# Attention row sums as pairs of slabs added on GpSimd, and value products in four query quarters: a change to a conditioned attention kernel

## What is computed

```
h   = gamma * ((x - mean) / sqrt(var + eps) * ln_g + ln_b) + beta     # gamma, beta: cond @ Wg.T + bg, cond @ Wb.T + bb
q, k, v = split(h @ Wqkv.T + bqkv)                                   # 16 heads of 32
att = softmax(q @ k.T) / sqrt(512)
h1  = concat(att @ v) @ Wp.T + bp + x
out = (the same conditioned layer norm of h1) + h1
```

## Time and profile before

| | us |
|---|---|
| median of three runs | 1585.34 |
| lowest, highest | 1584.9, 1586.55 |
| profiled execution | 1583.32 |
| its span, first to last instruction | 1581.7 |
| mean granted TensorE clock | 0.976 of full speed |

### The profile page before, as it was taken

The page is one execution under the profiler, slowest core; times in us unless marked ns, Lnnn a source line. Parts: engine busy times, 40 slices in busy tenths (PEclk is TensorE's granted clock), DMA queues, the critical chain, the costliest instruction groups (busy, mean ns, idle before and its releaser), DMA issues.

```text
span 1581.7 us, 28876 instructions
## 1 busy us (share of the span) xinstructions
PE 1468.6 (93%) x8756; PEld 832.5 (53%) x8756; DVE 945.9 (60%) x1697; ACT 655.1 (41%) x794; POOL 426.7 (27%) x523
## 2 busy tenths in 40 slices
PE   6998999999999999999999999999999999999733
PEld 4886645555554656555555556555444444344332
DVE  5336666565656566665656666565666665666145
ACT  3221444444444444444444444344444444445300
POOL 2442201111111233131423323121313231323357
PEclk9999999999999999999999999999999999999966
DMA  6799563645434676656454575556334242423142
GB/s 215 178 173 186 135 77 97 92 111 70 109 86 85 162 108 154 72 149 91 118 126 94 160 97 160 56 141 95 95 82 111 67 121 54 123 58 92 52 113 87
DMA packets 211534, 175.98 MB, mean 111 GB/s; under 512 B 102644, under 2 KB 177396, under 8 KB 211480
## 3 DMA queue, kind: packets, MB, share of 16 engines
q1 hardware_dynamic: 209176, 167.96, 50.6%
q0 software_dynamic: 2304, 7.34, 1.2%
HBM read 115.13 MB, written 59.31 MB: 110 GB/s over the span
## 4 chain that ended last, share of the span: by engine, by line
PE 79%; DVE 7%; SPq 4%; issue 3%; DMA 3%; POOL 2%; ACT 1%; POOLq 1%; DVEq 0%; ACTq 0%
PE ps_o L673 19%; PE ps_a L638 16%; PE ps_st L653 11%; PE ps_w L545 9%; PE ps_o L670 9%; PE ps_w L602 8%; DVE half_max L993 5%; PE ps_st L602 3%; SPq L401 1%; PE ps_o L545 1%; PE ps_w L591 1%; DMA scale_t<-rcp_scratch 1%; PE ps_a L632 0%; POOL oT_s L1159 0%; SPq L356 0%
## 5 line engine op out<-in xcount | busy, mean ns | idle before, releaser
L993 DVE TENSOR_REDUCE half_max<-ps_a 128x1 f32<-128x512 f32 x1024 | 689.2, 689 | 484.0 <-PE ps_a L638 478.6
L809 ACT ACTIVATE p<-ps_st 128x1024 f32<-128x1024 f32 x512 | 521.9, 1025 | 499.4 <-PE ps_st L653 495.0
L670 PE MATMUL ps_o<-p,v_head 128*32 128x512 f32 x2048 | 490.2, 600 | 0.0
L673 PE MATMUL ps_o<-p,v_head 128*1 128x512 f32 x2048 | 483.5, 593 | 0.0
L638 PE MATMUL ps_a<-k_stack,q_stack 96*128 96x512 f32 x1024 | 429.4, 432 | 23.7 <-DVEq L1001 7.2
L653 PE MATMUL ps_st<-q_stack,k_stack 98*128 98x512 f32 x1024 | 328.7, 402 | 6.7 <-DMA q_stack<-max_rows 6.7
L638 PEld LDWEIGHTS ps_a<-k_stack,q_stack 96*128 96x128 f32 x1024 | 190.5, 188 | 256.1 <-DVE half_max L993 122.6
L653 PEld LDWEIGHTS ps_st<-q_stack,k_stack 98*128 98x128 f32 x1024 | 188.7, 191 | 40.8 <-issue 10.5
L602 PEld LDWEIGHTS ps_w<-hT_s,wqkv_s 128*128 128x128 f32 x1056 | 146.4, 188 | 47.4 <-issue 36.9
L602 PE MATMUL ps_w<-hT_s,wqkv_s 128*128 128x256 f32 x1056 | 158.0, 285 | 0.0
L673 PEld LDWEIGHTS ps_o<-p,v_head 128*1 128x1 f32 x2048 | 69.8, 82 | 154.8 <-issue 154.8
(11 more groups left out here) (86 smaller groups left out, 1017.9 us busy)
## 6 DMA issues: line engine op xcount, KB each, us to landing
qk_scratch<-qkT_s SPq DMA_DIRECT2D x108, 256.0 KB, 2.4
q_stack<-qk_scratch SPq DMA_DIRECT2D x192, 128.0 KB, 3.0
k_stack<-qk_scratch SPq DMA_DIRECT2D x192, 128.0 KB, 3.3
v_scratch<-v_parts SPq DMA_DIRECT2D x32, 264.0 KB, 10.7
v_head<-v_scratch SPq DMA_DIRECT2D x64, 132.0 KB, 2.2
x_tile<-in_x SPq DMA_DIRECT2D x32, 256.0 KB, 5.3
gq_s<-gain_bias_scratch SPq DMA_DIRECT2D x16, 512.0 KB, 4.9
att_scratch<-o_stage SPq DMA_DIRECT2D x128, 64.0 KB, 1.6
```

Of the source, the lines that this page charges most:

```text
L670: pe.matmul(ps_o[HD * e:HD * e + HD, :], v_head[:, s, k, 0:HD], p32[:, k, e * 512:(e + 1) * 512], start=(k == 0), stop=(k == 7))
L673: mm = pe.matmul(ps_o[64 + HD * e:65 + HD * e, :], v_head[:, s, k, HD:VP], p32[:, k, e * 512:(e + 1) * 512], start=(k == 0), stop=(k == 7))
L809: nc.scalar.activation(p32[:, k, :], scores, ACT.Exp).then_inc(exp_done, 1)
L993: V.tensor_reduce(half_max[:, s % 2, item:item + 1], ps_a[:, parity, :], AX.X, ALU.max).then_inc(a_used, 1)
```

## The change

It does the following.
1. **Row sums.** The column of sqrt(512) leaves V (`VP` goes, V is stored with 32 columns) and is a tile of its own, `root_s`. POOL adds slab `2j` to slab `2j + 1` in place in `p32`, 128 x 1024 (`pair_add`), four times a head, once the products of both slabs with V are done, at steps given by `PAIR_ADD_STEP`. PE multiplies each added pair with `root_s` (`pair_sums`) in a bank of its own, `ps_s`, four products of 256 queries. Pair 0's sums are at step `k = 7`, pairs 1, 2 and 3 at `k = 1, 3, 5` of the next head, ahead of the products with V.
2. **Values.** `weighted` makes four products of 256 queries a slab at the four partition groups of `ps_o`, where `sums` made two of 512 for V and two of 512 for the sums. Both slabs of a burst wait once.
3. **Scores.** `ps_st` has three banks of 512 columns where it had four. The two halves of a slab are separate: the first is issued where both were, the second after the second piece and all `a_item`s of the step, right before the burst. ACT takes two exponentials of 512 columns. A half waits for the exponential of the half three before (`ST_AFTER`), but the second half of a new head's first slab waits for the last half of the head before.
4. **Copies and stores.** `take_out` (256 columns, `k = 2`) and `take_sums` (256 columns, `k = 6`) for one copy of 512; four DMAs for the output, and four for the sums at `k = 7`.
5. **Tables.** Output projection at steps 21, 22, 25, 26 (was 23, 24, 27, 28), layer norm statistics of the second tile and POOL's norms earlier, reciprocals at step 9, output loads at step 12, residual loads at step 1.

```
-OUT_STAGE = {23: (0, 1), 24: (0, 2), 27: (1, 1), 28: (1, 2)}
-LN_STEP = {5: 0, 13: 1}
-OUT_STATS_STEP = {27: 0, 31: 1}
-NORM_SCALE_STEP = {7: 0, 15: 1}
-NORM_GAIN_STEP = {9: 0, 17: 1}
-RESIDUAL_STEP = {9: 0, 13: 1}
+OUT_STAGE = {21: (0, 1), 22: (0, 2), 25: (1, 1), 26: (1, 2)}
+LN_STEP = {5: 0, 9: 1}
+OUT_STATS_STEP = {25: 0, 29: 1}
+PAIR_ADD_STEP = {0: 2, 2: 3, 4: 0, 6: 1}
+RESIDUAL_STEP = {3: 0, 4: 1}
+NORM_SCALE_STEP = {7: 0, 11: 1}
+NORM_GAIN_STEP = {8: 0, 12: 1}
+OUT_NORM_STEP = {15: 0, 16: 1}
+OUT_LOW_STEP = {19: 0, 20: 1}
 OUT_SCALE_STEP = {27: 0, 31: 1}
-OUT_FINISH_STEP = {29: 0, 31: 1}
+OUT_FINISH_STEP = {28: 0, 31: 1}
-RECIP_STEP = 7
-RECIP_STORE_STEP = 8
-OUT_LOAD_STEP = 10
-OUT_NORM_STEP = {13: 0, 15: 1}
-OUT_HIGH_STEP = {16: 0, 18: 1}
-OUT_LOW_STEP = {18: 0, 20: 1}
+RECIP_STEP = 9
+RECIP_STORE_STEP = 10
+RESIDUAL_LOAD_STEP = 1
+OUT_LOAD_STEP = 12
+OUT_HIGH_STEP = {17: 0, 18: 1}
...
+        ST_BANK = [0, 1, 2] * 5 + [1]
+        ST_AFTER = [r - 3 for r in range(15)] + [13]
+        ST_AFTER[0:3] = [12 - 16, 15 - 16, 14 - 16]
...
-                need(pe, exp_done, 32 * g + 8 * s + k - 1)
-                for e in range(2):
-                    mm = pe.matmul(ps_st[:, k % 2, e, :], ...)
-                mm.then_inc(st_ready, 1)
+                need(pe, exp_done, 64 * g + 16 * s + ST_AFTER[2 * k + e] + 1)
+                pe.matmul(ps_st[:, ST_BANK[2 * k + e], :], ...).then_inc(st_ready, 1)
...
-                for e in range(2):
-                    pe.matmul(ps_o[HD * e:HD * e + HD, :], v_head[:, s, k, 0:HD], p32[:, k, e * 512:(e + 1) * 512], ...)
-                for e in range(2):
-                    mm = pe.matmul(ps_o[64 + HD * e:65 + HD * e, :], v_head[:, s, k, HD:VP], p32[:, k, e * 512:(e + 1) * 512], ...)
-                mm.then_inc(pv_done, 1)
+                for e in range(4):
+                    mm = pe.matmul(ps_o[HD * e:HD * e + HD, 0:QW], v_head[:, s, k, :], p32[:, k, e * QW:(e + 1) * QW], ...)
+                if k % 2:
+                    mm.then_inc(pv_done, 1)
+            def pair_sums(g, s, j):
...
+                pe.wait_ge(pair_added, 16 * g + 4 * s + j + 1)
+                for e in range(4):
+                    mm = pe.matmul(ps_s[HD * e:HD * e + 1, 0:QW], root_s[:], p32[:, 2 * j + 1, e * QW:(e + 1) * QW],
+                                   start=(j == 0), stop=(j == 3))
+                mm.then_inc(sum_done, 1)
...
+                n, k = 64 * i + 2 * step, step % 8
+                freed = 16 * i + 4 * (step // 8) + k // 2 - 3
+                for e in range(2):
+                    act.wait_ge(st_ready, n + e + 1)
+                    if e == 0:
+                        need(act, sum_done if k % 2 else pair_added, freed)
+                    nc.scalar.activation(p32[:, k, e * 512:(e + 1) * 512], ps_st[:, ST_BANK[2 * k + e], :], ACT.Exp
+                                         ).then_inc(exp_done, 1)
...
+            def pair_add(g, s, j):
+                pool.wait_ge(pv_done, 16 * g + 4 * s + j + 1)
+                G.tensor_tensor(p32[:, 2 * j + 1, :], p32[:, 2 * j, :], p32[:, 2 * j + 1, :], ALU.add).then_inc(pair_added, 1)
...
                 for step in range(32):
+                    s, k = step // 8, step % 8
+                    if k in PAIR_ADD_STEP:
+                        j = PAIR_ADD_STEP[k]
+                        if j < 2:
+                            pair_add(i, s, j)
+                        elif not (first and s == 0):
+                            pair_add(i - (s == 0), (s - 1) % 4, j)
```

More of the change, by code:

```diff
@@ L479, in iteration @@
                             store_row(u + 1, (s + 1) % 4)
+                        if k == 7 and not (first and s == 0):
+                            store_sums(u - 1, (s + 3) % 4)
+                        if outs and step == RESIDUAL_LOAD_STEP:
+                            for a in range(2):
+                                load_residual(pair, a)
                         if step == RECIP_STORE_STEP and not first:
@@ L515, in _ @@
             for half in range(2):
[L516 removed]
+                sp.wait_ge(att_out[half], 256 * ITERS)
             for a in range(2):
@@ L719, in iteration @@
                             a_item(*use)
[L720 to L723, removed]
+                        after = (i, s, k + 1) if k < 7 else (i + (s + 1) // 4, (s + 1) % 4, 0)
+                        if last and (s, k) == (3, 7):
+                            after = None
+                        if after:
+                            turned_scores(*after, 0)
                         piece(step - 1, 1)
@@ L726, in iteration @@
                             a_item(*use)
+                        if after:
+                            turned_scores(*after, 1)
+                        before = (i - (s == 0), (s - 1) % 4)
                         if k % 2:
+                            behind = not (first and s == 0)
+                            if k == 7:
+                                pair_sums(i, s, 0)
+                            elif behind:
+                                pair_sums(*before, (k + 1) // 2)
                             for j in (k - 3, k - 2):
                                 if j >= 0:
-                                    sums(i, s, j)
-                                elif not (first and s == 0):
-                                    sums(i - (s == 0), (s - 1) % 4, j + 8)
+                                    weighted(i, s, j)
+                                elif behind:
+                                    weighted(*before, j + 8)
                         piece(step, 0)
@@ L743, in _ @@
             iteration(ITERS - 1, False, True, last=True)
-            for k in (6, 7):
-                sums(ITERS - 1, 3, k)
+            for k in range(6, 8):
+                weighted(ITERS - 1, 3, k)
+            for j in range(1, 4):
+                pair_sums(ITERS - 1, 3, j)
             for m in range(END, ITERS):
@@ L831, in iteration @@
                     if k == 2 and not (first and s == 0):
+                        take_out(4 * i + s - 1, (s + 3) % 4)
+                    if k == 6 and not (first and s == 0):
                         take_sums(4 * i + s - 1, (s + 3) % 4)
```

96 lines of the change are left out of this document (54 added, 42 removed).

## The result

| | us |
|---|---|
| changed kernel, median of 4 runs (lowest, highest) | 1666.42 (1661.9, 1670.76) |
| kernel before, in the same runs | 1585.94 (1584.9, 1587.51) |
| ratio, 95% interval | 1.0506 (1.0474 to 1.0538) |
| span of the profiled execution, before and after | 1581.7, 1660.2 |

The change makes the kernel 5.1% slower, 80 us. The forecast was no change (1583), with a range that ended at 1619.

A forecast was written before the change was run, and what follows sets the result against it. PE was taken to set the time, though not wholly, with DVE's reductions pacing some pairs. From 1583.3 profiled, -78.7 + 50 + 10 + 3 + 13.5 = -2, median 1583 us; own range 1572 to 1596, with rivals 1545 to 1619.

The forecast's parts named there:

- POOL's adds: 256 additions of 128 x 1024 on POOL: 2.37 us each, POOL's busy time from 427 to some 1034 us.
- Burst: PE's products with V and row sums: 1.42 us to the next load, 0.43 saved in each of 256 bursts.
- DVE's pace: Step pairs without a long tile piece: limited by DVE's reductions, period 4.06 us, 0.21 saved in each of 127.
- What is left of the gain after exponentials and smaller parts: Whole kernel without POOL's losses: 78.7 us gain, less 10 for exponentials and 3 for the output projection's start.
- C: Iterations 11 to 15, with output projections alone: 75.8 us before, some 76 forecast, including 3.9 lost to POOL.
- so I take no change: Reciprocals two steps later, but Q and K stacks issued before them: no change, 2 us either way in five iterations.
- Exponentials: ACT's two exponentials of 512 columns: hidden except at step 7 of 11 iterations, 0.9 us each, 10 us lost.
- POOL late after iterations with outputs: PE waits at step 3 for POOL's late add: 5.1 us six times, 3.9 five times, 50 us lost.
- the tail: End of last iteration: 37.3 us from step 21's burst to the last product's end, 13.5 us later than before.
- POOL keeps up: Rival, 20%: an add on POOL may run at the one-input rate, 1.35 us, giving 1545 us.
- The adds are slow: Rival, 14%: POOL's adds take 3.3 us, giving 1619 us; it decides from an add of 2.5 us on.
- Issue bounds the burst: Rival, 12%: 24 loads 0.06 us apart make PE's burst 1.57 us, giving 1614 us.

The follow-up runs named there:

- e11: Kernel before, with the maxima's high and low parts made by DVE reductions, nothing else changed: 1594.3 us, ratio 0.9979.
- e8: Changed kernel with all DVE work on the maxima between SBUF operands done by reductions, POOL's adds kept: 1595.5 us, ratio 1.0020 to the kernel before.
- e7: Changed kernel without POOL's adds, PE summing both slabs of each pair itself: 1644.4 us, ratio 1.0345 to the kernel before.
- e1: Changed kernel without POOL's adds or waits for them, half of each row sum left out: 1518.2 us, ratio 0.9565 to the kernel before.
- e6: Changed kernel, maxima's high part by a reduction, second output tile's last two POOL instructions behind next iteration's step 0 add: 1661.5 us, ratio 1.0449.
- e9: e8 with the second output tile's last two POOL instructions moved behind the add of step 0 of the next iteration: 1550.9 us, ratio 0.9736.
- e10: e9 with those two POOL instructions moved further, behind the add of step 2: 1533.9 us, ratio 0.9607 to the kernel before.

## Why the prediction was wrong

**The step that failed** is in the part on POOL's adds: "I take 2.37, as most of DVE's work in the loop reads PSUM". The sentence asks how DVE slows POOL. It was right on that (2.38). It never asks how POOL slows DVE. The 128 small instructions per kernel between SBUF operands were in the trace, and one of them took 1.28 us where its median was 0.17, which is one POOL instruction. The groups by line that I read had them too, with means of 0.22 and 0.24 us. I drew nothing from them, and no term of the sum and no rival had them. With POOL at 27% of the span that hold was worth about 3 us (e11). With POOL at 62%, back to back for over 9 us just where the maxima are split, it is 77 (changed kernel less e8).

The Trainium skill, "GPSIMD Engine Reference", section "8. Key points", says that GpSimd "Shares its SBUF interfaces with VectorE" and names as contending the DVE instructions in a 2-port performance mode or with two SBUF inputs. The trace agrees on the subtraction and on the reductions (one input, never above 0.173 us), and the copy fits if it runs in such a mode, which no run shows. That section gives no size. Here the DVE instruction is not slowed by a share: it waits whole POOL instructions out, the one under way at least and in the worst cases five in a row.

**The other terms, by their steps:**
- *Burst* 1.42: 1.41. Two groups less are 0.45 us (e7 against e1), and 0.43 was taken.
- *DVE's pace*, a period of 4.06: 3.96, so 0.31 saved where 0.21 was taken.
- *What is left of the gain after exponentials and smaller parts*, without POOL's losses: 1519.5, and e1 has 1518.2. By iteration 80.4, 84.9 (90 less 5.1) and 72.1 (76 less 3.9), and e1 has 79.7, 84.9 and 73.4 to 75.3. C is above since the pair of steps 13 to 15 rose from 6.1 to between 6.8 and 8.1, and a burst at the lower clock follows it: PE waits for a maxima row behind the output loads, 13.2 us in all in e1 where 6.7 was before. That is where "so I take no change", on the moved loads and reciprocals, was wrong, by about 2 us an iteration.
- *Exponentials*, 0.9 at step 7: the pair of steps 5 to 7 went from 5.68 to 5.98 us where 0.43 should have gone, so 0.73.
- *POOL late after iterations with outputs*, 50: the mechanism was right, and PE's wait of 3.94 and ACT's of 4.19 at step 3 compare with 5.1 forecast. What the sum lacked was what follows the stop, 1.3 to 2.7 us more in the next pair in e8 at the lower clock. Together with the tail (36.7 us from the burst of step 21 to the last product's end, forecast 37.3) it is 1588.5 - 1516.3 = 72 us, against 63.5.

So 77 of the 149 us that the adds cost are the missed hold, and 72 the late chain, if the hold is removed first. The split depends on that order: with the finish moved, the subtraction's hold alone is worth 113 us (e6 less e9). In the changed kernel the two overlap: PE's wait for the adds is only 34.1 us there and 55.7 in e8, and one edit gained 5 us in e6 and 45 in e9. My reading is that the hold delays PE near the late adds and so gives POOL time; that is argued from these rows.

**The rivals.** "POOL keeps up" needed an add at 1.35 us; it took 2.38. "The adds are slow" set its threshold at 2.5 us an add, and they stayed below. It had the right pair of engines and the wrong victim. "Issue bounds the burst" wanted 1.57 us a burst, and 24 products with their loads took 1.41. The Trainium skill, "TensorE: Matmul & The Clock Gate", section "Wait — 56ns, not 53.3ns?", has about 62 ns a matmul with hardware decoding off, an estimate of 1.62 us a burst. The trace has 1.41, and no run shows which decoding is on.

## What to carry to other kernels

When work moves to GpSimd, list every VectorE instruction between SBUF operands and look at the longest of each, not at its mean: a copy or a two-input operation of eight columns can wait for the whole of GpSimd's unbroken run (up to 8.96 us here). A reduction did the same work without waiting in every run, and a difference of two neighbouring values can be written as one. Then look for the run itself, since one reordering was worth 5 us while the hold stood and 45 us once it was gone: remove the hold first, then judge the order.

## What the runs showed that was not expected

- A DVE copy or subtraction of 128 x 8 was held for up to 8.96 us, through several POOL instructions; the ends at 777.06 and 777.03 in iteration 7 are 0.03 us apart. Others got through at the first seam. Where the copy waited long, the subtraction behind it did not, and the other way round. Reductions never waited: those from SBUF took at most 0.173 us, those from PSUM 0.695.
- Stops of 1 to 4 us were followed by products at half the rate (a score product 0.63 us for 0.40; the burst's starts 2.11 us apart for 1.10), for a burst and sometimes the pair behind it. Not after each one: in e9 the stops at step 5 of iterations 5 to 10, 0.85 to 1.25 us long, all left the burst at 1.10, and in e10 one of 1.2 us did not. What decides it was not tried.
- A group of four concurrent float32 passes of 256 columns costs 0.22 us, half of one of 512 columns (0.43 in the earlier trace rows).
